# Attention block with FFN gate on one core: the reads of turned probabilities go by query block instead of by partition block

## The reference

```python
def _L0_attn_ref(x, Wq, bq, Wk, bk, Wv, bv, Wo, bo, gamma, beta):   # H, G, E = (16, 4, 128); KV = 4
    Q = (x @ Wq + bq).reshape(b, l, H, E)
    K = (x @ Wk + bk).reshape(b, l, KV, E)
    V = (x @ Wv + bv).reshape(b, l, KV, E)
    # K and V are repeated for the G = 4 query heads of each of the KV = 4 key heads
    scores = jnp.einsum('blhe,bmhe->bhlm', Q, K) / np.sqrt(E)
    attn = jax.nn.softmax(scores + causal_mask, axis=-1)
    ctx = jnp.einsum('bhlm,bmhe->blhe', attn, V).reshape(b, l, H * E)
    y = jax.nn.gelu(ctx @ Wo + bo, approximate=False)
    return layernorm(x + y) * gamma + beta
def _L0_ffn_ref(h, w_gate_up, w_down):          # 256 -> 2 x 1024 -> 256
    return (silu(h @ gate.T) * (h @ up.T)) @ w_down.T
xn = _layernorm(x)
return x + _L0_attn_ref(xn, ...) * _silu(_L0_ffn_ref(xn, ...))
```

## Time and profile before

| | |
|---|---|
| median of 3 runs | 639.62 us (638.48 to 640.6) |
| the profiled execution | 639.54 us |
| its span, first to last instruction | 637.8 us |
| TensorE busy | 604.4 us (95%), 3342 instructions |
| VectorE, ScalarE, GpSimd busy | 475.8, 428.4, 304.4 us |
| mean granted TensorE clock | 0.982 of full speed |
| DMA: packets, bytes, mean rate | 68918, 113.28 MB, 178 GB/s |
| share of 16 DMA engines, main queue | 62.5% |

### The profile page before, as it was taken

One profiled execution on the slowest core, in us unless ns is written; L12 is line 12 of the kernel. 1 busy time (PEld: TensorE's weight loads), 2 busy tenths in 40 slices (PEclk: granted clock), 3 DMA queues, 4 the chain that ended last, 5 costly groups with the idle time before them and its releaser, 6 DMA issues.

```text
span 637.8 us, 10638 instructions
## 1 busy us (share of the span) xinstructions
PE 604.4 (95%) x3342; PEld 523.9 (82%) x3342; DVE 475.8 (75%) x1122; ACT 428.4 (67%) x1023; POOL 304.4 (48%) x244
## 2 busy tenths in 40 slices
PE   8799999999799999999999999999999999999770
PEld 6688888888688888898978889898988989888650
DVE  6544556543888778888988788899878888987836
ACT  4334444534787787777978777698877869877540
POOL 1000000000055754645689655468975546898554
PEclk9999999999899999999999999999999999999796
DMA  8330132020497888966678987848798794979840
GB/s 274 115 120 33 67 99 66 1 74 20 136 242 208 218 227 251 246 206 166 173 192 250 262 231 208 239 138 227 232 273 237 194 251 128 240 206 289 222 111 33
DMA packets 68918, 113.28 MB, mean 178 GB/s; under 512 B 7552, under 2 KB 46592, under 8 KB 66816
## 3 DMA queue, kind: packets, MB, share of 16 engines
q1 hardware_dynamic: 68432, 112.30, 62.5%
q10 hardware_dynamic: 432, 0.33, 0.2%
HBM read 66.40 MB, written 46.20 MB: 177 GB/s over the span
## 4 chain that ended last, share of the span: by engine, by line
PE 79%; DMA 7%; DVE 6%; ACT 3%; issue 2%; POOL 1%; SPq 1%; ACTq 0%; DVEq 0%; POOLq 0%
PE bank L1027 32%; PE down_ps L1027 14%; PE down_ps L1177 12%; PE down_ps L1087 7%; PE bank L1056 6%; PE bank L1054 6%; DMA probs<-p_scratch 3%; DMA p_scratch<-probs 2%; PE bank L1138 2%; DMA raw<-in_wgu 2%; DVE probs L958 2%; ACT probs L704 1%; SPq L485 1%; POOL pT_lo L570 1%; DVE wgu_lo L807 1%
## 5 line engine op out<-in xcount | busy, mean ns | idle before, releaser
L570 POOL TENSOR_TENSOR pT_lo<-probs,pT_hi 128x512 fp32r<-128x512 f32 x160 | 204.3, 1299 | 79.2 <-ACT pT_hi L714 78.4
L704 ACT ACTIVATE probs<-probs,least 128x512 f32<-128x512 f32 (+3 forms) x256 | 141.0, 554 | 38.7 <-DVE least L935 38.1
L935 DVE CUSTOM_DVE_ANT_0 probs<-bank,mask 128x512 f32<-128x512 f32 (+3 forms) x256 | 117.7, 485 | 30.0 <-PE bank L1027 26.0
L582 POOL TENSOR_TENSOR probs<-probs,inv 128x1024 f32<-128x1024 f32 (+1 forms) x32 | 47.0, 1469 | 146.0 <-DVE inv L944 146.0
L714 ACT ACTIVATE pT_hi<-probs 128x512 fp32r<-128x512 f32 x160 | 96.5, 626 | 14.3 <-DMA probs<-p_scratch 7.6
L958 DVE STREAM_TRANSPOSE probs<-probs 128x2048 f32<-128x2048 f32 (+1 forms) x64 | 95.4, 1491 | 0.3 <-POOL probs L582 0.3
L1177 PE MATMUL down_ps<-wo_lo,cT_hi 128*128 128x256 f32 x256 | 74.3, 290 | 6.3 <-DVE cT_lo L983 6.2
L1177 PE MATMUL down_ps<-wo_hi,cT_lo 128*128 128x256 f32 x256 | 72.5, 283 | 0.0
L1177 PE MATMUL down_ps<-wo_hi,cT_hi 128*128 128x256 f32 x256 | 72.4, 283 | 0.0
L1027 PE MATMUL bank<-kT_lo,qT_hi 128*128 128x384 f32 (+1 forms) x192 | 66.1, 344 | 4.6 <-DVE least L935 3.5
L1027 PE MATMUL down_ps<-pT_lo,v_hi 128*128 128x512 f32 x160 | 65.2, 407 | 2.0 <-POOL pT_lo L570 2.0
(11 more groups left out here) (146 smaller groups left out, 1407.0 us busy)
## 6 DMA issues: line engine op xcount, KB each, us to landing
p_scratch<-probs SPq DMA_DIRECT2D x16, 1024.0 KB, 4.4
probs<-p_scratch SPq DMA_DIRECT2D x64, 256.0 KB, 5.0
p_scratch<-probs SPq DMA_DIRECT2D x16, 768.0 KB, 5.7
probs<-p_scratch SPq DMA_DIRECT2D x64, 192.0 KB, 4.2
inv_b<-i_scratch SPq DMA_DIRECT2D x32, 256.0 KB, 5.1
p_scratch<-probs SPq DMA_DIRECT2D x16, 512.0 KB, 3.0
probs<-p_scratch SPq DMA_DIRECT2D x64, 128.0 KB, 4.7
p_scratch<-probs SPq DMA_DIRECT2D x16, 256.0 KB, 4.7
```

The costliest lines, as they stand in the source:

```text
L570: nc.gpsimd.tensor_tensor(lo[:].rearrange("p (a n) -> p a n", a=BLOCKS), turned(t, j), f32(hi[:]).rearrange("p (a n) -> p a n", a=BLOCKS), ...
L582: nc.gpsimd.tensor_tensor(p, p, factor, ALU.mult).then_inc(probs_made, 1)
L704: nc.scalar.activation(p, p, ACT.Exp, bias=least[:, u, g:g + 1], scale=-1.0, accum_out=total[:, n * T + t, g:g + 1]).then_inc(exp_done, 1)
L935: nc.vector.tensor_tensor_reduce(out=head_of(t, g), in0=ps[:, 0:(t + 1) * P].rearrange("p (k i) -> p k i", i=BLOCK), in1=mask_of(t), scale ...
```

## The change

The four reads of a unit are cut another way. Before, read q takes, from all 128 rows in DRAM, the column part q, and fills the 32 partitions of block q, all columns. After, read a takes 32 whole rows in DRAM, those of block a, and fills column part a of all 128 partitions. The four together move the same elements to the same places. Semaphores and their counts are the same.

```diff
-    def turned_back(i, t, q):
+    def turned_back(i, t, a):
 
-        return p_scratch[i][t].rearrange("(a m) (q n) -> q m a n", a=BLOCKS, q=BLOCKS)[q]
+        return p_scratch[i][t].rearrange("(a m) (q n) -> a q m n", a=BLOCKS, q=BLOCKS)[a]
...
             elif kind == "R":
                 t = step[2]
                 sp.wait_ge(blocks_out[t], 16 * n + 16)
-                for q in range(BLOCKS):
-                    sp.dma_start(probs[t][q * BLOCK:(q + 1) * BLOCK].rearrange("p (a n) -> p a n", a=BLOCKS),
-                                 turned_back(n % 2, t, q)).then_inc(probsT_in[t], 16)
+                for a in range(BLOCKS):
+                    sp.dma_start(probs[t][:].rearrange("p (a n) -> p a n", a=BLOCKS)[:, a],
+                                 turned_back(n % 2, t, a)).then_inc(probsT_in[t], 16)
```

## The result

| | before | after |
|---|---|---|
| median of 4 runs | 640.11 us (638.48 to 641.0) | 840.30 us (839.71 to 842.07) |
| ratio | | 1.3117, 95% interval 1.3085 to 1.3149 |
| span of the profiled execution | 637.8 us | 838.8 us |
| TensorE busy | 95% | 79% |
| granted clock, mean | 0.982 | 0.908 |

Slower by 200 us, 31%; forecast were 866 us, in a range of 775 to 1010.

What follows compares the result with a forecast made beforehand. TensorE bounds the old kernel; after the change four DMA engines do, 39.8 + 2 = 41.8 us per period against 28.0. 639.54 us + 207 for fifteen intervals + 19.6 in the tail = 866 us, range 775 to 1010.

Steps and rivals of the forecast that it cites:

- What bounds the kernel: From first to last read of t=3: TensorE is the bound, busy 418.95 of 420.30 us; quicker reads can gain little.
- How many engines: Changed reads, 4 steps of q on the DRAM side: each runs on 4 DMA engines, all on the same four.
- The load: Four engines, per period: 876 KB on each at 22 GB/s, 39.8 us; bounds 35.2 and 50.9 us.
- What lies between: Turn-rounds W3 to R3 and W2 to R2 leave engines partly empty: 2 us (0 to 4) per period, making 41.8 us.
- The compute loop fits: From R2's landing to the next W3: W3 could be issued at 33, engines work until about 37, 4 us to spare.
- The tail: From R3 of period 15 to ScalarE's first instruction after R0: 37.7 us instead of 18.1, so 19.6 us more.
- Sixteen engines: Rival for the reads: all sixteen engines serve them; quicker, 634 us, chance 0.06, or nothing to see, 639 us, chance 0.05.
- The late compute loop with a lower clock: Rival in the periods: four engines, TensorE idles, clock falls, compute becomes late too; some 3 us more per period, 911 us, chance 0.15.
- the 45 us: Late-compute rival's extra time over the 15 periods: 15 x 3 = 45 us, giving 911 us; chance 0.15.
- The signs: In the changed profile: small packets 4480, reads without landing time, DMA share 0.42, TensorE 0.65, ScalarE waits of hundreds of us.

Runs made afterwards that it cites:

- the runs with quicker reads: Kernel before with the scratch laid out anew and each write cut in four: four reads of one source run each 647.64 us, one read per unit 647.51 us.
- the pairs kernel: The change with each read cut into two of 64 partitions, 2 steps of q instead of 4: 1265.5 us, ratio 1.975 to the kernel before.
- one read per unit: New scratch layout, write cut into four, one read of 128 partitions x 4 runs per unit instead of four reads: 647.51 us, ratio 1.009 to the kernel before.
- The kernels with t=3 and t=2: Kernel before with only units t=3 and t=2 read by query block: 820.78 us; the same with three exponentials moved ahead in ScalarE's list: 795.91 us.

## Why the prediction was right, point by point

- *What bounds the kernel.* TensorE at 418.95 of 420.30 us left nothing to gain; the runs with quicker reads confirm it, 647 us.
- *How many engines.* Four, as worked out from the packet count: 7552 became 4480, forecast 4480. By the Trainium skill's rule ("DMA: Bandwidth & Descriptors", "Why a DMA increments its semaphore by 16 and not by 1") the trace agrees; in addition the pairs kernel shows two engines for two steps, and the stretch at 637 us and the sums over all reads show that they are always the same.
- *The load.* 22 GB/s were taken, 22.2 measured; 39.8 us, and it was 39.5. To take the fast beginnings of the reads rather than the mean of 17.2 was right. The reason given, that sixteen engines are slow when they share 32 partitions, holds in part: with one read per unit, when a read of t=3 fills all 128 partitions, sixteen engines move 397 / (1.03 x 16) = 24.1 GB/s each (433.3 to 435.3 us, the beginning of a write among them). But the mean of that kernel's periods is still only 218 / (0.75 x 16) = 18.2, so something else slows sixteen engines too, and that 22 fitted so closely is partly luck.
- *What lies between.* 2 us were added, 0.8 is left. This is the term that was mis-sized most: 1.2 of the 1.55 us per period (the load has the other 0.3), and the 1.55 are 23 of the 26 us by which the forecast was too long. With a rate good to 0.3 GB/s the 0.8 is good to half a us. The gap after W2 is there, with the share at 0.13 from 631 to 633 us, but it is short. That transfers issued ahead fill more of the time than I allowed is the likely reason; no run tests it.
- *The compute loop fits, "with 4 us to spare".* For the whole change it fits: the writes wait 15.7 us in all for VectorE. The 4 us were an error of the same step: I compared the time at which W3 can be issued (33) with the end of R0 (37), and left out the 4.7 us until W3 has landed, without which R3 can't start. The loop is 16 + 11 + 5.9 + 4.7 = 38 us long, 2 us from the bound. This error was harmless here only because those 2 us were left. The kernels with t=3 and t=2 show what that means: with less load they stay near it, at 39.0.
- *The tail.* 19.6 us more were forecast; from R3 of period 15 to the end it is 61.4 instead of 45.9 us, 15.5 more. 610.00 us was misread: by ScalarE's list (ph1.0, ph1.1, then ph0.0) that instruction waits for R1, and the one for unit 0 starts at 612.37, 20.5 us behind R3. In the changed kernel it starts at 814.36, 37.0 us behind R3, where the sum had 37.7. So the time to come was right, and the time now was 2.4 us too short. The first read is 2 us later; no changed read has run by then, and this start lies between 171.6 and 174.0 us in all kernels that write a unit in one transfer. 15 x 12.25 + 15.5 + 2 = 201, the difference of the spans.
- *The rivals.* Sixteen engines: out. The late compute loop with a lower clock: the clock does fall, to a mean of 0.91 in the periods. In the one shown TensorE is idle from 625 to 629 us, and the granted clock is 0.50, the lower level, from 627 to 635. The price is as the rival had it: TensorE is busy for 476.38 us where the same work took 418.95, 3.8 us per period. But the work lies under the transfers, and the 45 us did not come in the time.
- *The signs.* The packet count, the missing time to landing, the DMA share (0.43, forecast 0.42) and ScalarE's waits came. TensorE's busy share was forecast as 0.65 and is 0.79: the 418.95 us of work in a shorter period make 0.69, and the lower clock the rest.

## What to carry to other kernels

Before an access pattern is recut, look at the slowest dimension of both sides: if it has 4 or 2 steps, the transfer runs on 4 or 2 DMA engines (the cases measured here), and all such transfers on SyncE's queue share the same ones. The packets under 512 bytes in a trace tell it (each transfer leaves one closing packet per engine that it used), and so does a missing time to landing. A mean DMA share of 0.43 can then hide four full engines: work out the bytes on the busiest engine, and beside them the loop of waits through the transfer. The period was never shorter than the load; where the load was well above the loop it was the load, and where the two were close it lay above both (34.6 us, with about 31 for either).

## What was unexpected of the hardware

- Issuing slows down when few engines are loaded. A read takes 662 ns to issue in the median, and up to 2881, where it took 432 and at most 1553:

```profile
L485 SPq DMA_DIRECT2D probs<-p_scratch x256: 502/662/2881, 173.6 to 808.2; - x128
```

SyncE's queue accounts for 35% of the chain that ended last. Even transfers that use all sixteen engines, W0 or inv_b, wait behind it. That the queue runs full is the likely reason; no run shows it.
- A read on four engines is hurt less than fourfold. Sixteen engines that fill the same 32 partitions ran at 12.4 GB/s each in the later part of a group, four that fill 32 each at 22.2. R3, 1.05 MB, is in place 13.7 us after its first issue instead of about 7 (an estimate from its issue and landing rows).
- Moving two ScalarE instructions of 0.6 us behind three others cost the kernel before 43 us, 7%.
